# Attention and experts in one kernel: keys folded before their split, an exponential without scale, a router ranked in two parts, a last batch in two halves

## The reference, cut to what matters

```python
xn = layernorm(x)
# attention
q, k, v = xn @ Wq, xn @ Wk, xn @ Wv
latent = (k + v) @ W_down_kv
scores = clip(heads(q) @ heads(latent @ W_up_k).T / (sqrt(128) + 1e-8), -1e4, 1e4)
scores = clip(scores * exp(-1e-4 * |i - j|), -1e4, 1e4)
a = (softmax(scores) @ heads(latent @ W_up_v)) @ Wo
# experts
w, idx = top_2(xn @ Wr.T + br);  w = softmax(w)
y = sum over e of (w where idx == e) * (gelu(xn @ W1[e].T + b1[e]) @ W2[e].T + b2[e])
out = x + a + layernorm(y + xn) * ln_w + ln_b
```

## Time and profile before

| | |
|---|---|
| median of 3 runs | 271.71 us (271.5 to 272.08) |
| the profiled execution, its own time | 271.68 us |
| its span, first to last instruction | 269.4 us |
| mean granted clock of PE | 0.97 |
| busy: PE, PE's weight loads | 225.9 us (84%), 122.7 us (46%) |
| busy: ACT | 200.8 us (75%) |
| busy: DVE | 196.0 us (73%) |
| busy: POOL | 182.2 us (68%) |

### The profile page before, as it was taken

How to read it: one execution, slowest core, us unless ns; L and a number is a source line. 1 busy time by engine, 2 the same in 40 slices (tenths; PEclk the granted TensorE clock), 3 DMA queues, 4 the chain that set the end, 5 groups by cost and what they waited for, 6 DMA issues and landing times.

```text
span 269.4 us, 5034 instructions
## 1 busy us (share of the span) xinstructions
PE 225.9 (84%) x1673; PEld 122.7 (46%) x1673; DVE 196.0 (73%) x466; ACT 200.8 (75%) x335; POOL 182.2 (68%) x186
## 2 busy tenths in 40 slices
PE   0794557989999999998888888998788999999964
PEld 0572143879989899995122212222112231232313
DVE  2837986788988986874787876686967677667641
ACT  2557526445555565659999999999899999999950
POOL 9176708747787855594999999998899999700000
PEclk9998968999999999999999999999999999999995
DMA  6995601432217237311640169211890000000001
GB/s 202 438 439 202 175 22 39 133 134 79 67 53 179 68 74 188 78 27 49 184 112 23 29 164 217 61 29 33 207 202 2 1 21 20 0 39 2 1 39 45
DMA packets 17900, 27.46 MB, mean 102 GB/s; under 512 B 3008, under 2 KB 14944, under 8 KB 17488
## 3 DMA queue, kind: packets, MB, share of 16 engines
q1 hardware_dynamic: 15264, 22.21, 26.9%
q0 software_dynamic: 2272, 4.66, 7.4%
q10 hardware_dynamic: 336, 0.25, 0.4%
HBM read 13.01 MB, written 4.65 MB: 66 GB/s over the span
## 4 chain that ended last, share of the span: by engine, by line
PE 36%; ACT 29%; DVE 17%; issue 14%; DMA 2%; DVEq 2%; ACTq 0%
ACT shared L900 25%; PE ps L641 9%; PE ps L652 9%; PE ps L717 4%; PE ps L702 3%; DVE ps L1155 3%; PE ps L679 2%; PE ps L561 2%; DMA wvl<-w_router 2%; DVE shared L1016 2%; DVEq L1033 1%; PE ps L729 1%; DVE panels L1138 1%; DVE out_heads L1162 1%; PE ps L630 1%
## 5 line engine op out<-in xcount | busy, mean ns | idle before, releaser
L900 ACT ACTIVATE shared<-ps,rest_sb 128x1024 f32<-128x1024 f32 x128 | 130.1, 1153 | 1.7 <-DVE ps L1155 1.1
L1155 DVE TENSOR_TENSOR ps<-ps,mend_sb 128x256 f32<-128x256 f32 (+1 forms) x128 | 70.7, 562 | 29.8 <-PE ps L702 28.6
L869 ACT ACTIVATE shared<-ps,shared 128x128 f32<-128x128 f32 x156 | 44.5, 369 | 33.3 <-PE ps L641 33.3
L717 PE MATMUL ps<-shared,v_sb 128*9 128x512 f32 x512 | 66.9, 595 | 2.0 <-DVE out_heads L1162 1.2
L357 POOL DMA_INDIRECT shared<-xn_scr,source_i x39 | 46.5, 1192 | 29.4 <-PE ps L630 17.4
L702 PE MATMUL ps<-stacked 64*128 64x512 bf16 x256 | 49.6, 386 | 12.7 <-ACT shared L900 11.8
L702 PEld LDWEIGHTS ps<-stacked 64*128 64x128 bf16 x256 | 12.3, 92 | 81.4 <-ACT shared L900 73.7
L1036 DVE COPY shared<-panels 128x1156 f32 x39 | 38.8, 996 | 11.1 <-issue 10.8
L641 PE MATMUL ps<-shared 128*128 128x128 f32 x312 | 41.8, 277 | 2.4 <-DVE shared L1104 2.3
L652 PE MATMUL ps<-shared 128*128 128x128 f32 x312 | 41.5, 276 | 0.3 <-ACT shared L869 0.3
L641 PEld LDWEIGHTS ps<-shared 128*128 128x128 f32 x312 | 37.9, 192 | 3.6 <-DVE shared L1104 3.6
(11 more groups left out here) (156 smaller groups left out, 247.3 us busy)
## 6 DMA issues: line engine op xcount, KB each, us to landing
stacked<-parts SPq DMA_DIRECT2D x72, 128.0 KB, 2.6
panels<-weights SPq DMA_DIRECT2D x1, 4624.0 KB, 17.7
y_scr<-y_rows SPq DMA_DIRECT2D x19, 128.0 KB, 1.8
x_sb<-x_tiles SPq DMA_DIRECT2D x4, 256.0 KB, 4.7
xn_scr<-x_sb SPq DMA_DIRECT2D x1, 1024.0 KB, 9.0
xnT<-x_tiles SPq DMA_DIRECT2D x1, 1024.0 KB, 4.9
out<-panels SPq DMA_DIRECT2D x4, 256.0 KB, 2.0
shared<-xn_scr,source_i POOLq DMA_INDIRECT x39, 3.1
```

Source lines behind the costliest of these rows:

```text
L717: last = nc.tensor.matmul(ps[32 * g:32 * g + VW, OUT_BANK, :], v_sb[:, b * QT + tile, h, :], probs_fast[:, duo % DUO_SLOTS, g // 2, g % 2, :],
L869: last = nc.scalar.activation(hidden[:, i % 2, c, :], ps[:, i % 2, c * P:(c + 1) * P], ACT.Gelu, bias=panel[:, i % 4, 2 * F + D + c:2 * F ...
L900: nc.scalar.activation(probs_fast[:, duo % DUO_SLOTS, couple, :, :], ps[:, score_bank(n):score_bank(n) + 2, :], ACT.Exp, scale=key_fold[:, ...
L1155: nc.vector.tensor_tensor(both, both, mend_sb[:, mends].unsqueeze(1).to_broadcast([P, 2, mends.stop - mends.start]), ALU.mult).then_inc(fa ...
```

## The change

1. *Keys are folded ahead of the split.* POOL multiplies k by the key's factor over all 512 positions (a third row of `fold`), then splits. A split has ten steps, five for q and five for k. `key_fold` leaves the array `rest`; the array `fold` grows from 512 to 768 KB.
2. *The exponential has no scale.* Line 900 is `Exp` of the mended scores.
3. *The router is ranked in two parts.* `vl_psum` is signalled after tile 6 and after tile 16; DVE adds the bias to and ranks tiles 0 to 5, then tiles 6 to 15. ACT copies the values of two banks after the first signal and of four after the second.
4. *The last batch ends in two query halves.* The last group leaves the loop. Its copy of heads, turn, division, transposes, ACT's copy, projection, addition and DMA out are done for 256 queries each, first half and second half in turn on each engine, each in a PSUM bank of its own.
5. *Tokens are widened first.* In the expert loop of PE, `widen(n-1)` stands before `turn_places(n)`.

The diff, cut to its core:

```diff
@@ POOL, split_step(b, step) @@
+                side, at = divmod(step, 5)
+                kind, rows = ((RIGHT, qT_sb), (KEYS, kT_sb))[side]
+                into, ready = parts[:, b % 2, kind], parts_ready[kind]
+                done, folds = PARTS * b, 2 * (2 * b + side)
+                if at == 0:
...
+                    nc.gpsimd.tensor_tensor(folded[:], rows[:, b * S:(b + 1) * S], fold_sb[:, kind, :], ALU.mult).then_inc(pool_step, 1)
...
-                elif step == 5:
-                    pool.wait_ge(qk_ready, 2 * b + 2)
-                    if b >= 2:
-                        pool.wait_ge(rows_in[KEYS][b % 2], STACKED * (b // 2))
-                    nc.gpsimd.tensor_copy(keys[:, 0, :], kT_sb[:, wide]).then_inc(parts_ready[KEYS], 1)
...
@@ POOL, close(splits) @@
                     if splits:
-                        split_step(2 + b, each)
+                        for n in range(each, SPLIT_STEPS):
+                            split_step(2 + b, n)
@@ ACT, attention @@
                     nc.scalar.activation(probs_fast[:, duo % DUO_SLOTS, couple, :, :], ps[:, score_bank(n):score_bank(n) + 2, :],
-                                         ACT.Exp, scale=key_fold[:, tile:tile + 1]).then_inc(fast_probs, 1)
+                                         ACT.Exp).then_inc(fast_probs, 1)
@@ PE, values(b) @@
-                if b == B - 1:
-                    last.then_inc(vl_psum, 1)
+                    if t + 1 in ROUTED:
+                        last.then_inc(vl_psum, 1)
@@ PE, expert loop @@
             for n in range(WORK + 1):
+                if n >= 1:
+                    widen(n - 1)
                 if n < WORK:
                     turn_places(n)
-                if n >= 1:
-                    widen(n - 1)
@@ ACT, values @@
-            act.wait_ge(vl_psum, 1)
-            act.wait_ge(logits_ready, 1)
-            for bank in range(VL_BANKS):
-                keep_values(bank)
+            for part, (first, last) in enumerate(((0, 2), (2, VL_BANKS))):
+                act.wait_ge(vl_psum, part + 1)
+                act.wait_ge(logits_ready, part + 1)
+                for bank in range(first, last):
+                    keep_values(bank)
@@ DVE, router @@
+            for part, tiles in enumerate((slice(0, ROUTED[0]), slice(ROUTED[0], TILES))):
+                v.wait_ge(vl_psum, part + 1)
+                if part == 0:
+                    add_router_bias(slice(0, 2), VL_TILES).then_inc(logits_ready, 1)
+                else:
+                    add_router_bias(slice(VL_BANKS - 1, VL_BANKS), TILES - (VL_BANKS - 1) * VL_TILES)
+                    add_router_bias(slice(2, VL_BANKS - 1), VL_TILES).then_inc(logits_ready, 1)
+                v.wait_ge(logits_ready, part + 1)
+                top_one(tiles, logits[:, tiles, :], top[:, 0, tiles], first[:, tiles, :])
...
+                top_one(tiles, logits[:, tiles, :], top[:, 1, tiles], second[:, tiles, :])
+                nc.vector.tensor_tensor(sel[:, tiles, :], first[:, tiles, :], second[:, tiles, :], ALU.add).then_inc(sel_ready, 1)
@@ PE, behind the attention loop (DVE, ACT and SP alike) @@
+                for half in range(2):
+                    pe.wait_ge(fast_heads, GROUPS + half)
...
+                    for t in (2 * half, 2 * half + 1):
+                        last = nc.tensor.transpose(ps[:, LAST_TURN[half], t * P:(t + 1) * P], out_heads[:, t * P:(t + 1) * P], ident)
+                    last.then_inc(fast_outT, 1)
...
+                for half in range(2):
+                    pe.wait_ge(attnT_ready, B + half)
+                    for t in (2 * half, 2 * half + 1):
+                        last = nc.tensor.matmul(ps[:, LAST_PROJECTION[half], t * D:(t + 1) * D], attnT[:, TILES - QT + t, :], wo_sb,
+                                                start=True, stop=True)
+                    last.then_inc(wo_psum, 1)
```

More of the change, by code:

```diff
@@ L46 @@
 STACKED = len(PRODUCTS) * 16
+SPLIT_STEPS = 10
 TOP = 2
@@ L90, in build @@
         rest_sb = sb("rest_sb", [P, REST_WIDE])
-        wq_cols, wo_sb, b_router, ln_w, ln_b, below, counting, place, earlier, tile_of, starts, head_ones, ranking, key_fold = (
+        wq_cols, wo_sb, b_router, ln_w, ln_b, below, counting, place, earlier, tile_of, starts, head_ones, ranking = (
             rest_sb[:, a:z] for a, z in REST.values())
@@ L297, in split_step @@
             def split_step(b, step):
-                queries, keys = parts[:, b % 2, RIGHT], parts[:, b % 2, KEYS]
-                wide, done = slice(b * S, (b + 1) * S), PARTS * b
-                if step == 0:
+                side, at = divmod(step, 5)
[3 more added lines that the diff above has]
+                if at == 0:
                     pool.wait_ge(fold_in, 2 * 16)
-                    pool.wait_ge(qk_ready, 2 * b + 1)
-                    if b:
+                    pool.wait_ge(qk_ready, 2 * b + side + 1)
+                    if side:
+                        pool.wait_ge(parts_ready[RIGHT], done + PARTS)
+                    elif b:
@@ L337, in split @@
             def split(b):
-                for step in range(9):
+                for step in range(SPLIT_STEPS):
                     split_step(b, step)
@@ L503, in _, with store @@
             sp.wait_ge(rows_in[LEFT][1], STACKED)
+            def store(tiles, count):
+                sp.wait_ge(out_ready, count)
+                sp.dma_start(out[:, tiles, :], z[:, tiles, :]).then_inc(stored, 16)
             with sp.If(fast == 1):
@@ L511, in _ @@
                         stack_rows(b, LEFT)
+                for b in range(B - 1):
+                    store(slice(b * QT, (b + 1) * QT), b + 1)
+                for half in range(2):
+                    store(slice(TILES - QT + 2 * half, TILES - QT + 2 * half + 2), B + half)
+                sp.wait_ge(stored, (B + 1) * 16)
             with sp.Else():
@@ L891, in _ @@
                     duo, couple = divmod(n, 2)
-                    tile = duo % QT
                     act.wait_ge(fast_fixed, n + 1)
@@ L900, in _ @@
                     nc.scalar.activation(probs_fast[:, duo % DUO_SLOTS, couple, :, :], ps[:, score_bank(n):score_bank(n) + 2, :],
-                                         ACT.Exp, scale=key_fold[:, tile:tile + 1]).then_inc(fast_probs, 1)
+                                         ACT.Exp).then_inc(fast_probs, 1)
+                for half in range(2):
+                    tiles = slice(2 * half, 2 * half + 2)
+                    act.wait_ge(attnT_psum, B + half)
+                    nc.scalar.copy(attnT[:, TILES - QT + tiles.start:TILES - QT + tiles.stop, :],
+                                   ps[:, LAST_ATTENTION[half], :].rearrange("p (t f) -> p t f", t=QT)[:, tiles, :]).then_inc(attnT_ready, 1)
             with act.Else():
@@ L988, in _, with add_router_bias @@
-            top_one(logits[:], top[:, 0, :], first)
-            then(nc.vector.scalar_tensor_tensor(logits[:], first, -3.0e38, logits[:], ALU.mult, ALU.add))
-            top_one(logits[:], top[:, 1, :], second)
-            nc.vector.tensor_tensor(sel[:], first, second, ALU.add).then_inc(sel_ready, 1)
+            def add_router_bias(banks, count):
+                tiles = slice(banks.start * VL_TILES, (banks.stop - 1) * VL_TILES + count)
+                many = banks.stop - banks.start
+                return nc.vector.tensor_tensor(
+                    logits[:, tiles, :].rearrange("p (a k) e -> p a k e", k=count),
+                    ps[:, banks, 0:count * VL].rearrange("p a (k w) -> p a k w", w=VL)[:, :, :, D:VL],
+                    b_router[:, None, None, :].to_broadcast([P, many, count, EXPERTS]), ALU.add)
@@ new lines, in top_one @@
+            def top_one(tiles, values, largest, onehot):
+                ranks, picked = top[:, 2, tiles], pick[:, tiles, :]
+                many = tiles.stop - tiles.start
+                rank = ranking.unsqueeze(1).to_broadcast([P, many, EXPERTS])
+                wide = lambda ap: ap.unsqueeze(2).to_broadcast([P, many, EXPERTS])
+                then(nc.vector.tensor_reduce(largest, values, AX.X, ALU.max))
+                then(nc.vector.tensor_tensor(picked, values, wide(largest), ALU.is_equal))
+                then(nc.vector.tensor_tensor(picked, picked, rank, ALU.mult))
+                then(nc.vector.tensor_reduce(ranks, picked, AX.X, ALU.max))
+                then(nc.vector.tensor_tensor(onehot, rank, wide(ranks), ALU.is_equal))
@@ L1263 @@
         head_ones=np.eye(HEADS, NORM_ROWS, dtype=np.float32)[by_dim(np.repeat(np.arange(HEADS), HD)[None])[0]],
[L1264 to L1265 removed]
+        ranking=spread(EXPERTS - experts))
     at = np.arange(S, dtype=np.float32)
```

114 lines of the change are left out of this document (59 added, 55 removed).

## The result

| | before | after |
|---|---|---|
| median (lowest to highest) | 271.87 us (271.5 to 272.08) | 276.1 us (275.72 to 277.89) |
| the profiled execution, its span | 271.68, 269.4 us | 276.38, 274.3 us |

The ratio is 1.017, with a 95% interval of 1.0123 to 1.0217: the changed kernel is slower by 4.6 us by the ratio, 4.2 by the medians. 269.0 us with a range of 266.9 to 270.5 was forecast, so the sign was wrong too.

What follows compares the result with a forecast made beforehand. ACT's exponential was taken to bound the kernel, with POOL's sum deciding at batch 2. From 271.68 us: before attention -0.4, batch 2's wait +0.1, units behind -2.1, last exponential -0.1, clock +1.5, end -1.7, giving 269.0 (266.9 to 270.5).

Steps and rivals of the forecast that it cites:

- the order inside this cycle changes no sum: PE's expert loop: widening before turning would gain 0.1 us, between -0.4 and +0.4.
- 39 times 0.1: Expert loop: the loss in us over its 39 rounds if narrow no longer covered DVE's copy.
- long waits for line 1104's copy: Expert loop: the sign that would show the forecast for the order of widening wrong; no size given.
- The router and the start: Before attention: ranking in two parts would gain 0.3 us, between -0.6 and +1.5.
- half of the late one is exposed: Router's second part: by the skill's shared-interface rule half is exposed to POOL, so the gain could be nil.
- The exponential: Attention, line 900: without scale, starts fall from 0.997 to 0.905 us apart and the duration to about 1.01 us.
- the prediction's 0.05 us: Exponential without scale: gain per unit by the skill page's 0.946 us, instead of the 0.09 us forecast.
- POOL's queue: Attention: tenth split steps delay POOL's chain by 2.76 us, so its third sum ends at 202.04 instead of 199.28.
- The hole: Ahead of unit 76: DVE waits over 4 us for POOL's batch 2 sum; the first 78 units lose 0.16 us.
- The clock: Behind batch 2's hole: PE idles about 4.7 us, then runs at 1.2 GHz for some 3.5 us, costing 1.5 us.
- 0.44 for each us: Attention behind the hole: the loss in us for each us that PE's clock stays at 1.2 GHz.
- The end: After the last heads' copy: two query halves would gain 1.7 us, between 1.5 and 2.2; the 2.0 us landing stays.

Runs made afterwards that it cites:

- e2: before with only the expert loop's order changed (widen, then turn): 277.79 us, ratio 1.0227.
- e9: e2's order of widening first on before, without POOL's four `ln_b` additions in the expert loop: 272.07 us, ratio 1.0017.
- e10: before, in its old order, without POOL's four `ln_b` additions in the expert loop: 269.02 us, ratio 0.9888.
- e3: before with only the keys folded by POOL and the exponential without its scale: 272.89 us, ratio 1.0046.
- e6: e1 with DVE's statistics four units later (58, 68, 85, 97) and the router ranked whole as in before: 269.41 us, ratio 0.9901.
- e5: e1 with the statistics at units 58, 68, 85, 97 and the exponential given a scale again, a column of ones: 271.96 us, ratio 1.0008.
- e7: before with only the last batch ended in two query halves: 270.79 us, ratio 0.9961.
- e11: before with only the router ranked in two parts: 271.36 us, ratio 0.9966.
- e1: after with the expert loop's old order put back (turn, then widen): 270.95 us, ratio 0.9962.
- e8: e1 with DVE's statistics moved behind a group's heads, `STATS_AT` 62, 70, 86, 102 for 54, 64, 75, 93: 264.32 us, ratio 0.9735.

## Why the prediction was wrong

**The step that failed** is "the order inside this cycle changes no sum", with its reason "where DVE is late, PE waits for the same copy in either order" and its 0.1 us, between -0.4 and +0.4. The first wait is the same in either order. What differs is what comes after it: in the old order the next turned tile is there already, so DVE makes up its delay at 1.1 us a tile; in the new one it cannot go below 1.63. The sum of the work doesn't change, the slack between stages does, from 2.0 to 0.9 us. It measured +6.0 us in after, +6.3 alone in e2. The small wait of the earlier trace rows was read as a proof that the copy isn't critical; it showed only that the slack covered it. The prediction's fallback, 39 times 0.1 for a copy that narrow no longer covers, was of the wrong kind as well, since e9 and e10, and the nine equal rounds near the loop's end, show that the loss sits where DVE is late. Its list of signs did name the right one, long waits for line 1104's copy, but no rival had it.

**The router and the start**: -0.3 was forecast, +0.8 measured, of which +0.4 is the change's. The thirteen early operations fitted into DVE's idle time and the late ones took 0.24 us each, both as forecast. Mis-sized was POOL beside them. Two operations were blocked for 1.0 us each; "half of the late one is exposed" was too little. By the Trainium skill, "GPSIMD Engine Reference", section "1. Specifications", the interfaces are shared when VectorE has two SBUF inputs or runs in a 2-port mode. As far as the inputs go, the trace agrees: the reduction of before at 22.29 with one input kept its 0.29 us beside POOL's multiplication, and the products did not. But the operation at 29.25 has one input as well and took 1.04 us, for 0.18 of a like one just before; whether it ran in such a mode no run here shows. Nor does everything of POOL count, as the early operations took 0.21 us each beside its memset. That the tenth step would reach into the sort stood nowhere in the prediction; without the router's parts it costs 0.9 us there (e3, e6). Inside the traces the parts are worth 0.4 us alone and 0.5 beside the folded keys; the times say 0.9 and 1.2 to 2.35, with scatter and clock in them. The sign was right.

**The exponential** was right in its price. Its median is 1.03 us and its shortest 0.997, against 1.01 forecast; starts were 0.90 to 0.91 us apart. The price rested on a fixed part of 0.06 us that no row shows, so some of that is luck. A plain group took 7.5 us, against 7.47, but not every group gained: the two in which DVE also splits q (units 4 to 11 and 20 to 27) took 8.4 and 8.3 us, as in before. By the Trainium skill, "ScalarE: Activation LUTs", section "What ACT_TABLE_LOAD costs", a unit is 0.946 us, which is longer than the starts of after; the same section puts each [128,1] pointer operand at 93 ns, a price that the prediction's 0.05 us leaves out and with which the trace agrees (0.10 us, e5).

**POOL's queue** was right: the third sum was to end at 202.04; with the 6.8 us by which attention starts later that is 208.8, and it ended at 208.90. **The hole** came out right in size, in part by luck. The waits of "about 1 us each" for the sums of batches 0 and 1 did not come (no idle time stands before their statistics), and the 75 units ahead of batch 2's gained 3.9 us instead of 5.3 (9.3 groups at 0.57), as two groups gained nothing. The two errors pull opposite ways. DVE waited 4.06 us for "over 4", and the first 78 units together were 0.24 us slower than before, for 0.16.

**The clock** fell as forecast, to 0.50, though already within PE's idle time of 3.99 us. It stayed there for 7 us, twice the 3.5 of the earlier trace rows; before has such a long stretch as well, from 35.1 to 41.9 us, ahead of its loop. By the prediction's own 0.44 for each us, 6.8 us would lose 3.0, or 2.1 without the 2.0 in which PE was idle. The units behind the hole gained 0.5 us, for 0.7 forecast: the sum of plain gain and clock was near, and how it splits between the two no run shows.

**The end**: 1.7 was forecast and 1.6 measured, but for a mixed reason. The stretch from the heads' copy to the last addition was forecast as 4.7 us at the lower clock or 4.0 at the full one; it was 3.99 at the full one. In the earlier trace rows the clock had fallen, and this part of the difference belongs to the clock: at the same clock the halves bring some 0.5 us (e7). The landing did not stay as it was: from the last addition to the end of the span are 3.1 us instead of 2.5.

The measured terms make up the span: +0.8 + 6.0 - 0.3 - 1.6 = +4.9 us. With -0.1 in place of +6.0 and -0.3 in place of +0.8, it would have been the forecast's -2.7 within 0.4. By the runs one at a time: e2 +6, e3 +1, e7 and e11 -1 each make about +5.

## What to carry to other kernels

In a loop in which engines hand work to each other, count for each handed-over tile how long the consumer's engine is busy with other things between the two uses: this slack, and not the sum of the work, decides what a late partner costs, and a small wait in the profile says only that it has sufficed so far. When one engine gets faster, look for the waits in its neighbours' queues that were met by a few us, and move them in the order before counting the gain: here the four numbers of `STATS_AT` were worth 6.6 us (e1 to e8), more than all the rest of the change. Look also for which operations of POOL will fall beside which of DVE's after the change, since each such meeting cost about 1 us here, with POOL's instructions 1.2 to 1.3 us long.

## What the runs showed of the hardware

A short DVE operation that falls beside a POOL `tensor_tensor` can last until that one ends: 1.29 and 1.20 us for 0.24 beside 1.26 and 1.15, 1.04 for 0.18 beside 1.16, 1.23 for 0.17 beside 1.05. A weight copy took 2.37 us with a gather and an addition of 1.29 beside it, and 1.01 with the gather alone. Reductions, with one input from SBUF, kept their time (0.29 us beside 1.27), and so did the early part of the router beside POOL's memset (0.20 to 0.21 us each).

In the hole of after PE was idle for 3.99 us in the middle of steady work. Its clock fell 2.0 us into that and stayed at the lower level for 7 us, though PE was busy for 3.70 of the six that the window shows.

A `scale` that is a column in SBUF costs ACT 0.1 us in an exponential of 128x1024 from PSUM, with the column of ones in e5 (1.132 us, for 1.032 without) as with the factors of before (1.142).
